# Bringing the context in already turned, in place of eight transposes on TensorE and two copies out of PSUM in each sequence

## The reference

```python
def _fq(x, delta, zp, n_bits):                       # quantise and bring back
    xi = _round_ste(x / delta) + zp
    return (jnp.clip(xi, 0.0, 2.0 ** n_bits - 1.0) - zp) * delta

def _attn(x, ctx, wq, wk, wv, wo, bo, dq, dk, dv, dw):  # 16 heads of 32
    q = (x @ wq) ...;  k = (ctx @ wk) ...;  v = (ctx @ wv) ...
    sim = einsum(_fq(q), _fq(k)) * SCALE
    out = einsum(_fq(softmax(sim)), _fq(v))
    return out @ wo + bo

h1 = _ln(x, ln1_g, ln1_b)
x = _attn(h1, h1, a1_...) + x
h2 = _ln(x, ln2_g, ln2_b)
x = _attn(h2, context, a2_...) + x          # keys and values from the context
...                                         # feed-forward; then a second layer
```

## Time and profile before

| what | value |
|---|---|
| median of 3 runs | 2904.44 us |
| lowest, highest | 2903.19, 2906.63 us |
| span of the profiled execution | 2903.8 us |
| quantised stage, to the second stage's first DMA | about 1224 us |
| one round (one sequence) of the quantised stage | about 70.0 us |
| mean granted TensorE clock | 0.974 |

### The profile page before, as it was taken

How to read it: one execution, slowest core, us unless ns; L and a number is a source line. 1 busy time by engine, 2 the same in 40 slices (tenths; PEclk the granted TensorE clock), 3 DMA queues, 4 the chain that set the end, 5 groups by cost and what they waited for, 6 DMA issues and landing times.

```text
span 2903.8 us, 55443 instructions
## 1 busy us (share of the span) xinstructions
PE 2712.0 (93%) x18432; PEld 2209.4 (76%) x18432; DVE 1784.4 (61%) x4410; ACT 1454.0 (50%) x3765; POOL 710.5 (24%) x1147
## 2 busy tenths in 40 slices
PE   5799999999999998589999999999999999999997
PEld 4566666666666665279999999999988888888885
DVE  6789999999999997554344434445434434534533
ACT  4577777777777775431111111113355555555554
POOL 1222222222222221123222222222212212212211
PEclk9899999999999999789999999999999999999999
DMA  4343333334334332341111121215011111111111
GB/s 149 75 86 83 83 83 80 83 79 83 83 81 85 85 83 59 94 142 58 72 65 72 58 74 56 79 51 181 30 44 51 51 43 51 51 44 50 56 38 37
DMA packets 337324, 211.07 MB, mean 73 GB/s; under 512 B 275569, under 2 KB 291953, under 8 KB 337265
## 3 DMA queue, kind: packets, MB, share of 16 engines
q1 hardware_dynamic: 337264, 210.34, 27.2%
HBM read 92.84 MB, written 50.33 MB: 49 GB/s over the span
## 4 chain that ended last, share of the span: by engine, by line
PE 53%; DVE 2%; issue 1%; ACT 0%; DMA 0%; POOL 0%; SPq 0%; DVEq 0%; POOLq 0%
PE AG L157 33%; PE Y L157 12%; PE XT L1292 2%; PE O L1315 2%; PE XT L1302 2%; PE XT L132 1%; DVE parts L1636 1%; DVE xhat L124 1%; PE Y L132 0%; PE O L1325 0%; DVE turned L186 0%; ACT stage L1532 0%; DMA stage<-in_ff_w_dram 0%; DVE mid_parts L1693 0%; POOL base L1846 0%
## 5 line engine op out<-in xcount | busy, mean ns | idle before, releaser
L157 PE MATMUL AG<-h_parts,up 128*128 128x256 f32 x6144 | 779.4, 285 | 14.4 <-DVE down L1617 11.2
L157 PEld LDWEIGHTS AG<-h_parts,up 128*128 128x128 f32 x6144 | 763.3, 193 | 27.0 <-issue 11.9
L595 ACT ACTIVATE e<-S,bias,qk_scale 128x256 f32<-128x256 f32 x1024 | 563.1, 564 | 66.6 <-DVE e L707 62.5
L1861 POOL TENSOR_TENSOR mid_parts<-mid_act,mid_parts 128x256 fp32r<-128x256 f32 x256 | 199.7, 780 | 1080.4 <-DVE mid_parts L1693 1080.4
L1500 ACT ACTIVATE gate<-AG,cols_pack 128x256 f32<-128x256 f32 x256 | 121.5, 474 | 673.5 <-PE AG L157 673.0
L157 PE MATMUL Y<-down,mid_parts 128*128 128x512 f32 x1536 | 403.9, 400 | 0.0
L1686 DVE SCALAR_TENSOR_TENSOR mid_act<-AG,cols_pack,gate 128x256 f32<-128x256 f32 x256 | 123.4, 482 | 426.2 <-ACT gate L1500 425.3
L690 DVE TENSOR_REDUCE negmax<-S 128x4 f32<-128x1024 f32 x256 | 312.3, 1220 | 103.9 <-PE S L503 102.2
L157 PEld LDWEIGHTS Y<-down,mid_parts 128*128 128x128 f32 x1536 | 272.2, 189 | 68.7 <-issue 22.6
L707 DVE TENSOR_SCALAR e<-e,rsum 128x256 f16<-128x256 f32 x1024 | 292.0, 349 | 2.5
L565 ACT ACTIVATE shifted<-PJ,round_col,inv 128x512 f32<-128x512 f32 x192 | 149.2, 777 | 226.2 <-PE PJ L157 225.2
(11 more groups left out here) (132 smaller groups left out, 3832.1 us busy)
## 6 DMA issues: line engine op xcount, KB each, us to landing
stage<-in_ff_w_dram SPq DMA_DIRECT2D x48, 256.0 KB, 4.8
x_in<-in_x_dram SPq DMA_DIRECT2D x16, 512.0 KB, 3.8
ctx_in<-in_ctx_dram SPq DMA_DIRECT2D x16, 512.0 KB, 3.7
mid_dram<-x SPq DMA_DIRECT2D x16, 512.0 KB, 2.7
own<-mid_dram SPq DMA_DIRECT2D x16, 512.0 KB, 3.3
own<-in_ctx_dram SPq DMA_DIRECT2D x16, 512.0 KB, 3.5
h_dram<-h3T SPq DMA_DIRECT2D x16, 512.0 KB, 2.6
k_dram<-own SPq DMA_DIRECT2D x16, 512.0 KB, 2.6
```

Of the source, the lines that this page charges most:

```text
L157: last = nc.tensor.matmul(acc, lhs(l), rhs(r), start=(start and i == 0), stop=(stop and i == 2))
L595: nc.scalar.activation(e[:, s, i, :], S[s][:, i // 2, i % 2, :], ACT.Exp, bias=bias[:, s, i:i + 1], scale=qk_scale[:, ph.a:ph.a + 1], accu ...
L1861: nc.gpsimd.tensor_tensor(mid_parts[:, f % 2, 1, :], mid_act[:, f % 2, :], mid_parts[:, f % 2, 0, :], ALU.subtract).then_inc(mid_low_done, 1)
```

## The change

A second copy of the context is given to the program, in the order in which `ctxT` holds it (sequence, partition, chunk, token). The DMA that filled `ctx_in` with tokens on partitions now fills it with channels on partitions; its size is the same. The `ctxT` fills are gone from all tables. ScalarE and VectorE round `ctx_in` straight to the high part, at the place where they copied and rounded before; VectorE and GpSimd take the low part from `ctx_in`. Two semaphores of their own, `ctx_high_done` and `ctx_low_done`, replace the shared ones. The load of the next context now waits for the low part, where before it waited for the transposes.

```diff
         PHASE2_FILLS = {0: [("q1", 0)], 1: [("q1", 1)], 2: [("k1", 0)], 3: [("k1", 1)],
-                        4: [("ctxT", 0), ("ctxT", 1), ("o1", 0)], 5: [("o1", 1)], 6: [("v1", 0)], 7: [("v1", 1)]}
+                        4: [("o1", 0)], 5: [("o1", 1)], 6: [("v1", 0)], 7: [("v1", 1)]}
...
-                     4: both("ctxT") + [("k1@1", 1)], 5: [("v1@1", 0)], 6: [("v1@1", 1)]}
+                     4: [("k1@1", 1)], 5: [("v1@1", 0)], 6: [("v1@1", 1)]}
...
-        P_Y_FILLS = {0: both("ctxT"), 1: [("k2", 0)], 2: [("k2", 1)], 3: both("o1"), 4: [("v2", 0)],
+        P_Y_FILLS = {1: [("k2", 0)], 2: [("k2", 1)], 3: both("o1"), 4: [("v2", 0)],
...
+                self.ctx_at = {id(PHASE2_FILLS): 4, id(P_A_FILLS): 4, id(P_Y_FILLS): 0}.get(id(fills))
+                self.ctx_seq = 0 if stage == "first" else b + 1
...
-            ctx_in = sb(one, "ctx_in", [P, TT, D])
+            ctx_in = sb(one, "ctx_in", [P, KC, TOK])
...
-                elif kind == "ctxT":
-                    seq = 0 if stage == "first" else b + 1
-                    pe.wait_ge(ctx_loaded, 16 * (seq + 1))
-                    ins = transpose_chunks(PJ[bank], ctx_in, j)
...
-                    pe.wait_ge(turned_low_done, 2 * turned_before(*where, ("ctxT",) if from_ctx else ("hT", "h2T")))
+                    if from_ctx:
+                        pe.wait_ge(ctx_low_done, 2 * (1 if stage == "first" else b + 2))
+                    else:
+                        pe.wait_ge(turned_low_done, 2 * turned_before(*where))
...
+            def wait_ctx(eng, ph, prev):
+
+                eng.wait_ge(ctx_loaded, 16 * (ph.ctx_seq + 1))
+                if prev is not None:
+                    wait_filled(eng, at(prev.stage, prev.b, "v2", 1))
+
+            def act_ctx_high(act, ph, prev):
+                wait_ctx(act, ph, prev)
+                nc.scalar.copy(ctxT[:, 0, 0:2, :], ctx_in[:, 0:2, :]).then_inc(ctx_high_done, 1)
...
+                    if g == ph.ctx_at:
+                        act_ctx_high(act, ph, prev)
                     act_exp(act, ph, g)
...
-                if kind_of(name) == "ctxT":
-                    nc.vector.tensor_copy(turned[:, 2:4, :], PJ[1][:].rearrange("p (c n) -> p c n", c=2)).then_inc(
-                        pj_emptied[1], 1)
...
+            def dve_ctx(dve, ph, prev):
+                wait_ctx(dve, ph, prev)
+                nc.vector.tensor_copy(ctxT[:, 0, 2:4, :], ctx_in[:, 2:4, :]).then_inc(ctx_high_done, 1)
+                dve.wait_ge(ctx_high_done, 2 * (ph.ctx_seq + 1))
+                nc.vector.tensor_tensor(ctxT[:, 1, 2:4, :], ctx_in[:, 2:4, :], ctxT[:, 0, 2:4, :],
+                                        ALU.subtract).then_inc(ctx_low_done, 1)
...
+            def pool_ctx_low(pool, ph):
+                pool.wait_ge(ctx_high_done, 2 * (ph.ctx_seq + 1))
+                nc.gpsimd.tensor_tensor(ctxT[:, 1, 0:2, :], ctx_in[:, 0:2, :], ctxT[:, 0, 0:2, :],
+                                        ALU.subtract).then_inc(ctx_low_done, 1)
...
-                    def load_ctx(seq, where):
-
-                        wait_filled(sp, where)
-                        sp.dma_start(ctx_in[:], ctx_v[seq]).then_inc(ctx_loaded, 16)
+                    def load_ctx(seq, done):
+
+                        sp.wait_ge(ctx_low_done, done)
+                        sp.dma_start(ctx_in[:], t["ctxT"][seq]).then_inc(ctx_loaded, 16)
...
+    a["ctxT"] = np.ascontiguousarray(a["ctx"].reshape(B, TOK, KC, P).transpose(0, 3, 2, 1))
```

More of the change, by code:

```diff
@@ L291, in phase1, with turned_before @@
             return Phase(0, n, stage, b, fills, (base + 3, base + 4), base + 6, (stage, b, "o2", 1))
-        TURNED = ("hT", "h2T", "ctxT")
-        def turned_before(stage, b, name, j, kinds=TURNED):
+        TURNED = ("hT", "h2T")
+        def turned_before(stage, b, name, j):
             def those(s, fills=None):
@@ L304, in turned_before @@
                 n += len(those("peeled"))
[L305 to L308, removed]
+            return n + len(those(stage, ORDER[stage][:ORDER[stage].index((name, j))]))
         WEIGHTS = ("a1_wq", "a1_wk", "a1_wv", "a2_wk", "a2_wq", "a2_wv")
@@ L538, in pe_phase @@
                     for name, j in fills:
-                        if kind_of(name) in ("hT", "h2T", "ctxT"):
+                        if kind_of(name) in ("hT", "h2T"):
                             pe_fill(pe, at(ph.stage, ph.b, name, j))
@@ L545, in pe_phase @@
                     for name, j in fills:
-                        if kind_of(name) not in ("hT", "h2T", "ctxT"):
+                        if kind_of(name) not in ("hT", "h2T"):
                             pe_fill(pe, at(ph.stage, ph.b, name, j))
@@ L577, in act_transposed @@
                     act.wait_ge(turned_low_done, 2 * n)
-                if kind_of(name) == "ctxT":
[L579 to L583, removed]
-                wait_emptied(act, where)
-                nc.scalar.copy(parts_of(where)[:, 0, 0:2, :], turned[:, 0:2, :]).then_inc(turned_high_done, 1)
+                i = "2" if kind_of(name) == "h2T" else "1"
+                affine_act(turned, PJ[0], 0, cols[f"ln{i}_g"], cols[f"ln{i}_b"], pj_emptied[0])
+                wait_emptied(act, where)
+                nc.scalar.copy(hT[:, 0, 0:2, :], turned[:, 0:2, :]).then_inc(turned_high_done, 1)
+            def wait_ctx(eng, ph, prev):
[5 more added lines that the diff above has]
+                nc.scalar.copy(ctxT[:, 0, 0:2, :], ctx_in[:, 0:2, :]).then_inc(ctx_high_done, 1)
             def act_exp(act, ph, g):
@@ L611, in late @@
                     return []
-                return [at(p.stage, p.b, n, j) for n, j in p.steps(s) if kind_of(n) not in ("hT", "h2T", "ctxT")]
+                return [at(p.stage, p.b, n, j) for n, j in p.steps(s) if kind_of(n) not in ("hT", "h2T")]
             def transposed(ph, g, j):
                 return [at(ph.stage, ph.b, n, i) for n, i in ph.steps(g)
-                        if kind_of(n) in ("hT", "h2T", "ctxT") and i == j]
+                        if kind_of(n) in ("hT", "h2T") and i == j]
             def act_phase(act, ph, prev):
@@ L820, in pool_beside_max @@
                 pool.wait_ge(prob_quantised, ph.group(g) - 1)
-            def pool_turned_low(pool, where):
-                n = turned_before(*where)
-                pool.wait_ge(turned_high_done, 2 * (n + 1))
-                parts = parts_of(where)
-                nc.gpsimd.tensor_tensor(parts[:, 1, 0:2, :], turned[:, 0:2, :], parts[:, 0, 0:2, :],
-                                        ALU.subtract).then_inc(turned_low_done, 1)
+            def pool_ctx_low(pool, ph):
+                pool.wait_ge(ctx_high_done, 2 * (ph.ctx_seq + 1))
+                nc.gpsimd.tensor_tensor(ctxT[:, 1, 0:2, :], ctx_in[:, 0:2, :], ctxT[:, 0, 0:2, :],
+                                        ALU.subtract).then_inc(ctx_low_done, 1)
             def pool_phase(pool, ph, nxt):
                 for g in range(GROUPS):
-                    if g >= 1 and ("ctxT", 0) in ph.steps(g - 1):
+                    if ph.ctx_at is not None and g == ph.ctx_at + 1:
                         pool_beside_max(pool, ph, g)
-                        pool_turned_low(pool, at(ph.stage, ph.b, "ctxT", 0))
+                        pool_ctx_low(pool, ph)
                     if ph.a == 1 and (ph.early or ("o1", 1) in ph.steps(5)) and g in (2, 3):
@@ L943, in _ @@
                         2: [lambda: load_two_chunks(3)],
-                        5: [lambda: load_ctx(1, ("first", 0, "ctxT", 1))], 6: [load_x_ahead]})
+                        5: [lambda: load_ctx(1, 2)], 6: [load_x_ahead]})
                     turn_phase(P_B, {6: [lambda: load_x(2, 2)]})
```

32 lines of the change are left out of this document (13 added, 19 removed).

## The result

| | before | after |
|---|---|---|
| device time, median (range, runs) | 2903.82 us (2901.65 to 2906.63, 4) | 2883.01 us (2877.99 to 2887.74, 4) |
| ratio after to before, 95% interval | | 0.993, 0.9917 to 0.9942 |
| profiled execution: time, span | 2904.44, 2903.8 us | 2880.16, 2878.4 us |
| granted TensorE clock of the profiled run | 0.974 | 0.975 |

The kernel is faster by 0.7%, 20.8 us at the medians. The predicted time was 4 us too low, inside its range. The two profiled spans differ by 25.4 us, which is the very sum of the prediction, but not of the same terms: one of them came out with the other sign. The first four times after lie 10 us apart, and of before 5. In larger sets the kernel of before spreads by 7 to 9 us too (2900.71 to 2911.37 over all its runs), so the 5 was a lucky draw; the changed kernel's 14 runs spread by 12.7.

The account below looks back on a forecast made before the run. TensorE was taken as the bound, with VectorE close behind. Rounds 17.1, `P_A` 3.0, `P_Y` 0.7 and clock 4.6 sum to 25.4 us; 2904.4 - 25.4 = 2879.0 us, range 2873 to 2888.

Parts of the forecast that it names:

- The rounds: Group 4 of thirteen loop rounds and the peeled one: TensorE saves 1.22 us each, 14 x 1.22 = 17.1 us.
- VectorE and ScalarE follow: Group 4: ScalarE keeps 0.6 us of slack; VectorE can come 1.16 us earlier against TensorE's 1.22, 0.06 late.
- `P_A`: Phase where TensorE idles 3.06 us ahead of the transposes for their bank: 3.0 us gained, bounds 2.2 and 4.4.
- VectorE's limit of 2.2 us: Lower bound in `P_A`: VectorE can give only waits of 0.88 and 0.64 us and its 0.69 copy.
- ScalarE's chain: Upper bound in `P_A`: shift to 69.0, rounding 0.6, four exponentials 2.2, so next scores at 71.9, 4.4 us less.
- `P_Y`: Phase where TensorE's 1.22 us are lost in waits and VectorE loses its copy: 0.7 us gained, bounds 0 and 1.2.
- The load and GpSimd: Context DMA (3.7 us) and GpSimd's low part: both covered, priced at nothing; 3.7 us a sequence if the DMA's cover were gone.
- The clock: Falls of TensorE's granted clock at the loop's `h2T` wait: three in place of seven, 4 x 1.16 = 4.6 us gained.
- the lock: Claim that clock falls in every second loop round are tied to the round's length (69.34 + 70.55), broken by cutting 1.22 us.
- one in every round: Rival: a clock fall in every round, 20.8 - 8.1 = 12.7 us gained, 2891.7 us; chance 0.10.
- the first rival: In the loop, the clock keeps its every-other-round falls, all else as forecast: 20.8 us gained, 2883.6 us; chance 0.20.
- Slower: Rival: clock falls behind both layer-norm waits, `h2T` and `hT`, 28 for 7, costing 24.4 us against 20.8: 2908.0; chance 0.03.

Follow-up runs that it names:

- the experiment: Changed kernel with six matmuls in each `h2T` wait, plus eight identity transposes put back in group 4 of `P_A` alone: 2877.25 us.
- the two other profiles: Profiles from two further timings of the changed kernel, nothing edited: medians 2880.65 us (4 runs) and 2883.16 us (6 runs).
- The filled pair: Kernel before and changed kernel, each with six matmuls of 512 columns put into the `h2T` wait of 14 rounds: 2897.6 and 2874.81 us.

## Why the prediction was right, and where it was not

**The rounds** were right. Predicted 1.22 us each and a quiet round of 68.12; measured 69.34 - 68.06 = 1.28, so 17.9 us in place of 17.1. Restoring the transposes alone brought back 1.17. The `h2T` wait stayed at 1.93 to 1.99, as foreseen. What I had not foreseen is the DMA wait of 1.47 us in the first round.

**VectorE and ScalarE follow**, as worked out: VectorE was to be 0.06 us late and is 0.05, and waits for scores in the next group. The copies put back cost nothing in a round. VectorE is 93% busy in a round (63.28 of 68.06 us) and that was still enough.

**`P_A`** was taken at 3.0 between bounds of 2.2 and 4.4; it measured 3.86, and 3.76 in the experiment. The step that was mis-sized is VectorE's limit of 2.2 us: I added its waits and its copy as if it had nothing else to give, but the transposes' return cost 3.76 without any copy on VectorE. Nearer the truth is ScalarE's chain (shift, rounding, exponentials), which I had put at 4.4: up to the scores of group 6, which wait for ScalarE, 4.56 us were gained. The scores of group 6 came at 70.89, below the 72 to 74 that I gave; they started from 64.72 in place of 65.60, and 6.17 us on.

**`P_Y`**: 0.7 taken, 0.71 measured.

**The load and GpSimd** at nothing: no wait on `ctx_in` appears, and its load takes 3.6 us.

**The clock** failed. I wrote that without the lock "I choose three falls in place of seven: 4 x 1.16 = 4.6 us gained". The profiled run had seven falls, which cost 7.8 us against 8.1, so 0.4 was gained in place of 4.6; the two other profiles had seven and five. The step that failed is the argument that a fall pushes what follows away from its place so that falls become rarer. Falls came in runs of up to four rounds, and their price is not one number, 0.8 to 2.1 us each by how long the clock stays down, so counting falls at 1.16 was wrong as well. That the alternation would break was right; that breaking it was a gain was not. What decides when a fall comes is still open. My range held because I kept seven falls and one in every round as rivals; by the time it was the first rival that came true, 2883.6 against 2883.0 measured, though not by its mechanism.

**The exact sum of 25.4 us** in the profile is a coincidence. Rounds 17.9, `P_A` 3.9 and `P_Y` 0.7 make 22.5. In the rounds the clock gives 0.4 and the DMA wait takes 1.5. The other 4.0 were not foreseen. 3.0 of them come ahead of the first `h2T`: 0.88 us before the first edited place (65.60 to 64.72), where the variants with the same code range from 64.48 to 67.28, and 1.6 in a projection of `P_B` that took 3.02 us in place of 4.61, at 1.00 in place of some 0.62; the rest is small differences in waits. 1.0 comes behind the last `h2T`. So the forecast of 2879.0, which lies within 2 us of the median of all 14 runs, owes this to luck: a clock term 4.2 us too high is made up by 1.7 us too little for the rounds and `P_A` and by the 2.5 us, 4.0 less 1.5, that it had no term for. The filled pair, 22.8 us apart, is the better measure of the change, and the three foreseen terms, 22.5, agree with it within its 1.5 us.

**Slower** (falls behind both waits) did not come. But the place was a possible one. With the `h2T` wait filled, every fall that is left lies behind `hT`: seven in the 78 rounds of the six profiles of such kernels. The profile with the copies has one there too, in its first round, with the `h2T` wait as it was.

## What to carry to other kernels

An instruction without a gap before and after it on the engine that bounds the kernel is worth its length from start to start, and one that waits for a bank is worth that wait too, as far as the next engine's chain allows: look there for the bound, not in the idle time of the engine that is merely busy. Read a round's time only from rounds at full clock, and count the clock's part by itself, as a spread rather than as a number; take out of it first what is an ordinary wait, as the 1.47 us here. If TensorE bounds the kernel and its clock falls at a regular wait, try filling that wait with spare work that ends before the wait does: here that was worth another 6 to 8 us, a third of what the change itself gave.

## What the runs showed of the hardware

- Equal waits of 1.93 to 1.99 us are accompanied in some rounds by a granted clock of 0.50 for up to some 6.5 us (the first 4 us behind 923.09 at 0.50, the next 4 at 0.69 in the mean), and in others by 1.00; which rounds differs between runs of one program (7, 7 and 5 of 13), and with it the time, from 2876.6 at a mean clock of 0.977 to 2889.3 at 0.969.
- With that wait filled, whether by six matmuls of 512 columns or by thirteen transposes, so that 0.39 or 0.36 us of it are left, no fall came at it in 78 rounds of six profiles. Seven came some 2.3 us behind the start of `hT`, where TensorE waits 0.71 and 0.76 us in quick succession, as it also does in the rounds without a fall.
- Transposes raise the clock as well as hold it: under 64 of them in a row it went from 0.50 to 1.00 with nothing else on TensorE.
- Thirteen transposes back to back took 1.64 us, 0.13 each in the mean, though one alone is recorded with 0.27: their cost in a stream is half of what one record says.
